# Routing of 15 of 16 token tiles moved from the expert stage into the last attention chunks of a one-core layer

## The reference

```
xn = layernorm(x) * gamma + beta
w = sigmoid(xn @ Wx @ Ww + bw); k = xn @ Wk; v = xn @ Wv; r = sigmoid(xn @ Wr)   # 8 heads of 64
state_t = (1 - w_t) * state_{t-1} + k_t v_t^T ;  y_t = r_t^T state_t
x1 = layernorm(x + y @ Wo)
logits = x1 @ gate_w.T                                  # 12 experts
top_w, top_i = top_k(softmax(logits), 2); top_w /= sum(top_w)
out = layernorm(x1 + sum_e  silu(x1 @ w1[e].T) * (x1 @ w3[e].T) @ w2[e].T * cw[:, e])
```

## Time and profile before

| | us |
|---|---|
| median of three runs | 822.91 (820.64 to 826.37) |
| the profiled execution, its own time | 822.39 |
| its span, first to last instruction | 820.5 |
| PE busy in the span | 730.4 (89%) |
| DVE, ACT, POOL busy | 501.1, 342.5, 312.5 |
| mean granted TensorE clock | 0.959 of full speed |

### The profile page before, as it was taken

One profiled execution on the slowest core, in us unless ns is written; L12 is line 12 of the kernel. 1 busy time (PEld: TensorE's weight loads), 2 busy tenths in 40 slices (PEclk: granted clock), 3 DMA queues, 4 the chain that ended last, 5 costly groups with the idle time before them and its releaser, 6 DMA issues. The chain is left out here.

```text
span 820.5 us, 17687 instructions
## 1 busy us (share of the span) xinstructions
PE 730.4 (89%) x6146; PEld 523.5 (64%) x6147; DVE 501.1 (61%) x1061; ACT 342.5 (42%) x688; POOL 312.5 (38%) x341
## 2 busy tenths in 40 slices
PE   5879899999999999999959971499999999999994
PEld 2658587886878868788636621366666666666641
DVE  4735968768587685876855558444444443444467
ACT  4455544646446464564375321122222222222254
POOL 0337554344554444544443102233443433444210
PEclk9999999999999999999969986699999999999997
DMA  8604443334433354323540249125555555722865
GB/s 341 248 2 155 154 154 105 104 104 155 155 104 104 103 156 155 116 91 104 154 154 29 76 148 364 51 66 192 185 191 187 192 201 208 265 79 89 274 251 205
DMA packets 39001, 126.64 MB, mean 154 GB/s; under 512 B 4000, under 2 KB 4384, under 8 KB 36768
## 3 DMA queue, kind: packets, MB, share of 16 engines
q1 hardware_dynamic: 32064, 103.31, 36.2%
q0 software_dynamic: 6880, 22.55, 8.2%
HBM read 81.02 MB, written 44.83 MB: 153 GB/s over the span
## 5 line engine op out<-in xcount | busy, mean ns | idle before, releaser
L854 DVE COPY_PREDICATED ST<-msk,pS 128x256 f32<-128x256 uint8 x224 | 121.1, 570 | 80.4 <-issue 51.1
L589 POOL TENSOR_TENSOR piece_parts<-piece,piece_parts 128x1024 f16<-128x1024 f32 x48 | 103.9, 2164 | 104.0 <-ACT piece_parts L534 104.0
L583 POOL TENSOR_TENSOR L<-L,AM 128x256 f32<-128x256 f32 x96 | 73.8, 769 | 109.4 <-ACT L L526 104.6
L1282 PE MATMUL pH<-ring,xgh 128*128 x344 | 104.2, 303 | 5.5 <-issue 3.0
L1283 PE MATMUL pH<-ring,xgh 128*128 x344 | 103.9, 302 | 0.0
L1284 PE MATMUL pH<-ring,xgl 128*128 x344 | 103.9, 302 | 0.0
L306 PE MATMUL pS<-L 64*128 64x64 f32 x1536 | 96.3, 271 | 0.0
L1616 POOL DMA_INDIRECT y_scratch<-ysb,sidx x43 | 42.9, 998 | 135.5 <-DVE ysb L1532 130.0
L1516 DVE TENSOR_TENSOR hid<-pH,sil 128x320 f32<-128x320 f32 x43 | 21.1, 492 | 119.5 <-ACT sil L1368 119.5
L567 DVE TENSOR_TENSOR L<-L,AM 128x256 f32<-128x256 f32 x96 | 72.8, 759 | 31.5 <-ACT L L513 29.9
L306 PEld LDWEIGHTS pS<-L 64*128 64x128 f32 x1536 | 91.1, 188 | 0.0
(11 more groups left out here) (239 smaller groups left out, 1673.5 us busy)
## 6 DMA issues: line engine op xcount, KB each, us to landing
piece<-in_w_experts SPq DMA_DIRECT2D x48, 512.0 KB, 5.1
w_split_scratch<-piece_parts SPq DMA_DIRECT2D x48, 512.0 KB, 3.9
ring<-w_split_scratch SPq DMA_DIRECT2D x12, 2048.0 KB, 8.7
yin<-y_scratch SPq DMA_DIRECT2D x16, 512.0 KB, 13.3
x_scratch<-X SPq DMA_DIRECT2D x1, 4096.0 KB, 14.4
out_x<-X SPq DMA_DIRECT2D x8, 512.0 KB, 2.8
X<-in_x SPq DMA_DIRECT2D x1, 3072.0 KB, 22.9
X<-in_x SPq DMA_DIRECT2D x2, 512.0 KB, 7.7
```

Source lines behind the costliest of these rows:

```text
L583: g.tensor_tensor(next_kept(k, lv, 0), kept(key, k, lv, 0), by, ALU.mult).then_inc(k_dec, 1)
L589: g.tensor_tensor(piece_parts[buf][:, 1, :], piece[buf][:, :], piece_parts[buf][:, 0, :], ALU.subtract).then_inc(piece_lo, 1)
L854: v.copy_predicated(out[:, :, :, 0 if lv == 0 else 1, :], msk[:, lv, :, :].rearrange(shape, m=m), pS[:, :, lv * S:(lv + 1) * S].rearrange( ...
L1282: pe.matmul(p[:, 0, 0:F], xgh[par][:, k, :], wh, start=(k == 0), stop=False)
```

## The change

1. `early`, a memory area of 32 KB for each partition, is shared: it holds the z and k weights first, then the routing's arrays (class `Routing`), later the diagonals of the mixing. pA lives through both blocks.
2. Weight pieces: 4 for each of chunks 0 to 11 (`LOT = 4`, pieces 2 and 3 both after level 6) and none in 12 to 15. ACT casts the fourth at the end of the chunk.
3. x1 is normalised in more and earlier parts (`X1_PARTS`): the root of tiles 0 to 7 at the end of chunk 9, their norms at the ends of chunks 10, 11, 12; tiles 8 to 11 in chunk 13, 12 in 14, 13 and 14 in 15. Each tile is stored by a DMA that ACT issues behind the next norm. Tile 15 is stored in the expert block.
4. Gating: the gate weights are padded to 32 columns and the four feature groups go to four column groups of PE side by side; a second step ("sum") adds them and gives the logits by token. Tiles 12 to 14 are gated alone with x as weights ("direct"). All 24 steps stand in chunks 13 to 15.
5. The top two of tiles 0 to 14 are found by DVE in chunks 14 and 15, the counts by PE behind chunk 15 (ahead of its `attend_out`), the ranks by DVE, and POOL makes 15 column one-hots at the end of the block.
6. The last chunk's state update, with `turn_keys` and `write_state`, is left out; its result is not used.
7. In the expert block only tile 15 is routed; the token number is multiplied into the column one-hots, one instruction for each tile and choice. Running sums of the tiles by expert come from one product and one reduction. The first four gathers use the address table in place.

```diff
-PIECE_AT = (4, 5, 6)
+PIECE_AT = {4: (0,), 5: (1,), 6: (2, 3)}
+UNITS = [u for q in range(3) for u in [("turn", q * GROUP + r) for r in range(GROUP)] + [("gate", q), ("sum", q)]]
+UNITS += [u for i in range(3 * GROUP, NT - 1) for u in (("turn", i), ("direct", i))]
+GATE_SLOTS = {NT - 3: [[0, 1], [2, 3], [4, 5, 6], [7, 8], [9, 10]], NT - 2: [[11], [12, 13], [14, 15], [16], [17, 18, 19]],
+              NT - 1: [[20], [21], [22, 23], [], []]}
+X1_PARTS = [(0, 8), (8, 12), (12, 13), (13, 14), (14, 15), (15, 16)]
+LATE_NORMS = {10: (0, 3), 11: (3, 6), 12: (6, 8)}
+NORM_SLOTS = {NT - 3: [range(8, 9), range(9, 11), range(11, 12)], NT - 2: [range(12, 13), [], []]}
-LOT = 3
+LOT = 4
+PIECED = 12
...
@@ PE, gate_step(u) @@
+                pe.wait_ge(gate_out, u - 1 if kind == "turn" and 2 <= u < SINGLE else u)
+                elif kind == "gate":
+                    for k in range(KT):
+                        t = pe.matmul(pA[GATE_W * k:GATE_W * (k + 1), bank, :], gw[:, k, :], xT[:, k, :], start=True, stop=True)
+                elif kind == "sum":
+                    for r in range(GROUP):
+                        t = pe.matmul(pA[:, bank, r * E:(r + 1) * E], logitT[:, r * P:(r + 1) * P], kc_col(kc, K_SUM),
+                                      start=(r == 0), stop=True, skip_group_check=True)
...
+            def count_tokens():
+                pe.wait_ge(gate_out, SINGLE)
+                pe.wait_ge(chosen_ready, 4)
+                pe.matmul(pA[:, 1, 0:(NT - 1) * E], ro.upper_h, ro.chosen[:, 0:NT - 1, :].rearrange("p n e -> p (n e)"),
+                          start=True, stop=True, skip_group_check=True)
+                for m in range(NT - 1):
+                    later = NT - m
+                    t = pe.matmul(pA[:, 1, (m + 1) * E:(NT + 1) * E], ro.ones_h,
+                                  ro.chosen[:, m:m + 1, :].broadcast_to([P, later, E]), start=False, stop=True, skip_group_check=True)
+                t.then_inc(count_full, 1)
...
+            count_tokens()
             attend_out(NT - 1)
...
@@ ACT, norm and chunk @@
+                if t:
+                    send_x2(t - 1)
+            def send_x2(t):
+                a.wait_ge(norm2, t + 1)
+                a.dma_start(x2_d[t * P:(t + 1) * P, :], X[:, t, :]).then_inc(x2_out, 16)
...
                 fill(4)
+                split(3)
+                if n == 9:
+                    root_x1(0)
+                if n in LATE_NORMS:
+                    a.wait_ge(stat2, 3)
+                    for t in range(*LATE_NORMS[n]):
+                        norm(t)
...
@@ DVE, chunk @@
+                if n == NT - 1:
+                    top_two(8, 12)
                 mask(n, k, 0)
...
                     add_out(n - 1)
+                if n == NT - 2:
+                    top_two(0, 4)
                 level(3)
...
+                if n == NT - 2:
+                    top_two(4, 8)
...
+            top_two(12, NT - 1)
             low_y(NT - 1)
+            ranks()
             add_out(NT - 1)
...
@@ POOL, end of the attention block @@
+            g.wait_ge(ranked, 1)
+            for n in range(NT - 1):
+                i = g.tensor_scalar(ro.oh_col[:, n, :], ro.col_h, ro.colf[:, 0, n:n + 1], tokens[:, n:n + 1], ALU.is_equal, ALU.mult)
...
@@ expert block, SP @@
-            sp.dma_start(x2_d.rearrange("(n p) c -> p n c", p=P), X[:, :, :]).then_inc(x2_out, 16)
+            sp.dma_start(x2_d[last * P:, :], X[:, last, :]).then_inc(last_out, 16)
...
@@ expert block, DVE (the four groups of tiles and L1435 to L1466 go) @@
+            v.tensor_copy(slot_h[:, :], kcol(K_SLOT))
+            columns(1, 0, last)
+            v.wait_ge(gate_full, 1)
+            step(v.tensor_copy(ro.logit[:, last, :], pO[:, 0, 0:E]))
+            step(v.max(ro.top[:, last, :], ro.logit[:, last, :]))
...
+            step(v.tensor_reduce(place[:, :, :], placed[:, :, :, :], AX.X, ALU.add))
+            columns(0, last, NT)
+            columns(1, last, NT).then_inc(col_ready, 1)
+            step(v.tensor_tensor(tile_h[:, :].rearrange("p (c n) -> p c n", c=2), place[:, :, :], ro.tilf[:, :, :], ALU.add))
+            for c in range(2):
+                at = slice(c * NT, (c + 1) * NT)
+                v.tensor_tensor(oh_tile[:, at, :], slot_h[:, :].rearrange("p (o n) -> p o n", o=1).broadcast_to([P, NT, SLOTS]),
+                                tile_h[:, at].rearrange("p (n o) -> p n o", o=1).broadcast_to([P, NT, SLOTS]), ALU.is_equal).then_inc(tile_ready, 1)
...
+            v.wait_ge(list_full, 1)
+            v.tensor_scalar(toki[:, :], pHT[:, 0, 0:SLOTS], -1.0, 0.0, ALU.add, ALU.max).then_inc(list_ready, 1)
...
@@ expert block, POOL @@
-            g.wait_ge(tile_ready, 1)
-            g.tensor_tensor(oh_tile[:, :, :], oh_tile[:, :, :],
-                            kcol(K_TOKEN, kh).rearrange("p (o n) -> p o n", o=1).broadcast_to([P, 2 * NT, SLOTS]),
-                            ALU.mult).then_inc(numbered, 1)
             g.wait_ge(list_ready, 1)
-            for k in range(AHEAD):
-                fetch(k, k, k + 1, first=True)
+            for k in range(AHEAD):
+                g.sem_inc(g_waited, 1)
+                g.indirect_dma_start(out=xg[k][:, :], out_offset=None, in_=x2_d,
+                                     in_offset=bass.IndirectOffsetOnAxis(ap=toki[:, k:k + 1], axis=0)).then_inc(x_in[k], 16)
```

More of the change, by code:

```diff
@@ L1243, in _ @@
-            for m in range(NT):
-                later = NT - m
-                t = pe.matmul(pG[:, 0, (m + 1) * E:(NT + 1) * E], ones[:, :],
-                              chosen[:, m:m + 1, :].broadcast_to([P, later, E]), start=False, stop=True, skip_group_check=True)
-            t.then_inc(count_full, 1)
-            pe.wait_ge(numbered, 1)
+            for k in range(KT):
+                t = pe.transpose(pX[:, 0, k * P:(k + 1) * P], X[:, last, k * P:(k + 1) * P], idt[:, :])
+            t.then_inc(gate_T, 1)
@@ new lines, in _ @@
+            pe.wait_ge(gate_T_out, 1)
+            for k in range(KT):
+                t = pe.matmul(pO[:, 0, 0:E], xT[:, k, :], gw[:, k, 0:E], start=(k == 0), stop=(k == KT - 1))
+            t.then_inc(gate_full, 1)
+            pe.wait_ge(last_chosen, 1)
+            for at, w in ((last, ro.upper_h), (NT, ro.ones_h)):
+                t = pe.matmul(pG[:, 0, at * E:(at + 1) * E], w, ro.chosen[:, last, :], start=False, stop=True, skip_group_check=True)
+            t.then_inc(total_full, 1)
+            pe.wait_ge(col_ready, 1)
@@ L1254, in _ @@
             t.then_inc(list_full, 1)
+            for n in range(NT, 2 * NT):
+                t = pe.matmul(pH1[:, 0, 0:SLOTS], ro.oh_col[:, n, :], oh_tile[:, n, :], start=(n == NT), stop=(n == 2 * NT - 1))
+            t.then_inc(second_full, 1)
             def turn(i, k, rounds):
@@ new lines, in _ @@
+            v.tensor_tensor(ro.chosen[:, last, :], ro.onehot[:, 0, last, :], ro.onehot[:, 1, last, :], ALU.add).then_inc(last_chosen, 1)
+            v.wait_ge(total_full, 1)
+            block_of = [pG[:, 0, i * E:(i + 1) * E].rearrange("p (o e) -> p o e", o=1) for i in (last, NT)]
+            v.tensor_tensor(ro.picked[:, :, last, :], ro.onehot[:, :, last, :], block_of[0].broadcast_to([P, 2, E]), ALU.mult)
+            step(v.tensor_scalar(counti[:, :], pG[:, 0, NT * E:(NT + 1) * E], float(P - 1), None, ALU.add))
@@ new lines, in _ @@
+            v.tensor_scalar(ro.tili[:, :, last:], ro.sloti[:, :, last:], P.bit_length() - 1, None, ALU.logical_shift_right)
+            step(v.tensor_reduce(tbase[:, :], before[:, :, :], AX.X, ALU.add))
+            v.tensor_copy(ro.colf[:, :, last:], ro.coli[:, :, last:])
+            base = tbase[:, :].rearrange("p (o e) -> p o e", o=1).broadcast_to([P, NT, E])
+            for c in range(2):
+                v.tensor_tensor(placed[:, c, :, :], ro.onehot[:, c, :, :], base, ALU.mult)
+            step(v.tensor_copy(ro.tilf[:, :, last:], ro.tili[:, :, last:]))
@@ L1594, in _, with fetch @@
         def _(g):
[L1596 to L1599 removed]
+            def fetch(i, k, steps):
+                g.wait_ge(xt_full, i - (AHEAD - 1))
                 g.tensor_copy(gidx[k][:, :], toki[:, bass.ds(i, 1)]).then_inc(g_step, 1)
```

487 lines of the change are left out of this document (251 added, 236 removed).

## The result

The changed kernel took 829.84 us in the median of 11 runs (827.81 to 835.01), the kernel before 822.91 in the median of 11 beside them. The ratio is 1.0088, with a 95% interval from 1.0057 to 1.012. The forecast was 812.7, in a range of 800 to 824: it had the kernel faster, and it became slower than the whole range. The profiled execution of the changed kernel took 831.66 us, its span 829.5, 9.0 more than the span of before.

What follows compares the result with a forecast made beforehand. PE was taken to bound the middle chunks (busy 273.4 of 280 us), a DVE chain the routing. The terms 10.0 - 1.9 + 2.7 - 20.5 = -9.7 against the profiled 822.4 us gave 812.7, range 800 to 824.

Steps and rivals of the forecast that it cites:

- fourth piece, up to chunk 13: Chunks 0 to 11: the extra weight piece delays chunk 0, odd chunks and chunk 11; PE pays 10.0 us before chunk 13.
- chunks 13 to 15, up to the mask: Chunk 13 wins 8.5 us, chunk 14 gives 6.6 back, chunk 15 keeps its length: last mask 1.9 us earlier.
- block's end: After the last mask: POOL's 15 column one-hots at 0.35 us each delay the routing; cost 2.7 us, upper bound 9.
- routing: Start of the expert block: with only tile 15 left, 40.4 us without expert matmuls become 19.9, a gain of 20.5.
- the walk: The prediction's step-by-step adding up of work and waits through the engines' queues, in the chunks and the routing.
- All of it shifts by 3.1: Chunk 0: the fourth cast delays wo_h and wo_l, level 0, key copy, kbT and PE's values by 3.1 us, bounds 0 and 3.5.
- the forecast of 0.8 each: Chunks 1, 3, 5, 7, 9: the extra cast delays kbT, for which PE already waits; 4.1 us in all, bounds 0 and 6.
- no wait of PE there is over 2 us: Chunks 13 to 15: PE's waits stay short, where before they were 3 to 4 us; argued against the clock falling.
- The gate of four column groups: Gating in chunks 13 to 15: each group overlaps only its neighbour's second pass, so 2.2 us a gate, bounds 0.9 and 3.6.
- The feared loss to DVE: Block's end: by the shared-port lock, POOL's columns can lose some 1.5 us to DVE, making the sum 814.2.
- Rival 3: Chunks 13 to 15: the clock falls to 1.2 GHz, 19 us more, 831.7 and slower than before; chance 0.10.
- Rival 2: Routing gain partly eaten at both ends: POOL columns at 0.6 (+3.7), gather held by ring loads (+3); 819.4; chance 0.20.

Runs made afterwards that it cites:

- e8: Changed kernel, but SyncE loads the third expert's weights into the ring only after the first gather of tokens has landed; one run took 830.71 us.
- e2: Changed kernel with three weight pieces in chunk 0, four in chunks 1 to 11 and one in chunk 12; 826.91 us, ratio to before 1.0045.
- e1: Changed kernel again, with only the loaded counts kept as 16-bit numbers and one short DVE step added; 828.79 us, ratio to before 1.0082.
- e9: Changed kernel, but in chunk 0 PE turns the same keys seven more times before reporting them, to stay busy in its wait; one run took 823.95 us.
- e6: Changed kernel with three weight pieces in all 16 chunks; 820.32 us, ratio to before 1.0009.
- e11: As e10, but a fourth weight piece only in even chunks from 2 to 12 and no pieces in chunks 14 and 15; 797.48 us, ratio to before 0.9693.
- e7: Changed kernel, but the second turn of the gating (unit 1) doesn't wait for ACT's copy of unit 0; one run took 822.46 us.
- e5: Changed kernel, but in chunk 14 the third gate and its sum precede the second half's values; tile 12's direct gate moves to chunk 15; 820.65 us, ratio 0.9994.
- e4: Changed kernel, but in chunk 14 PE writes the state update three more times while waiting for the second mask; 829.34 us, ratio to before 1.0077.
- e10: Changed kernel with the edits of e6, e7, e5 and e8, and the column one-hots shared between POOL and DVE; 816.61 us, ratio to before 0.9947.

## Why the prediction was wrong, step by step

Predicted and measured against the span of before, in us. T and T' are the ends of the last mask, as in the prediction: 474.98 and 494.20.

```
                                  predicted   measured
fourth piece, up to chunk 13         +10.0      +15.4
chunks 13 to 15, up to the mask       -1.9       +3.8
block's end                           +2.7       +9.0
routing                              -20.5      -18.8
rest                                     0       -0.5
sum                                   -9.7       +9.0
```

**Routing: near.** `toki` came 12.07 us after the block's start, the walk said 12.1; `oh_tile` at 9.05, the walk had 8.7. What was short is the gather: from its issue to the first expert matmul 8.4 instead of 7.2. e8 gives a part of the cause: without the third ring load the gather was 2.1 shorter and the first matmul 0.8 earlier. The walk had charged the ring loads with 0.5 us.

**Fourth piece: mechanism right, size too small, one effect left out.** "All of it shifts by 3.1": in e2 against e1 it was 4.3. The fourth cast began 5.67 us after its load was issued (64.42, then 70.09); the walk's 70.5 allows 4.7, less than its own row of 5.1. With its row the shift would have been 3.5; it was 4.0 on ACT and 4.3 behind POOL. The step that failed is that nothing was said of what PE does behind the wait: 3.8 us of clock in chunk 0.

In the odd chunks the forecast of 0.8 each was near: PE's wait for kbT went to 1.43 in chunks 1, 3, 5 and 7, and chunks 1 to 8 lost 2.2 together. (The five waits of before that the walk counted, in 120 to 400 us, are those of chunks 3 to 11 and not 1 to 9; the sum is the same.) For chunk 9 it was wrong by its clock. There PE waited 2.24 us for kbT, and of the 12 matmuls of `attend_out` eight then ran 0.43 apart instead of 0.22: 4.36 us from the first to the values, 2.68 in e9 where the wait was 1.45. For chunk 11 the walk had 2.8, and chunks 10 and 11 together lost 3.4: the late `normalise` that it foresaw came (the wait of 1.82 us at 365.67), and some 1.6 of the 3.4 are the clock behind that wait, by eight transposes and `read_state` at the low level. e6 and e11 show the late norms to be nearly free where chunk 11 has three pieces.

**Chunks 13 to 15: the step that failed is the walk's "no wait of PE there is over 2 us".** There were two, of 3.04 and 3.45 us. The first comes from a condition that I had in the diff before me and read as meant, not as written: for `u = 1` it falls through to `else u`. The first turn's copy stands on ACT behind kbT, three key copies and four state operations. e7 gives its price, 4.5 us; as chunk 13 even so won 7.4 of the 8.5 forecast, other terms of the walk there were too dear, and which is open. The second I had seen as a wait for the mask, but not that it stands in front of four units. I put 28.5 us from first mask to first mask for chunk 14, and it was 32.49 (446.55 to 479.04): 4.0 of the 5.7 by which this line of the table is off. e5 shows that the order alone, with the clock that comes with it, is worth 11.6.

The gate of four column groups was the one term on the other side: 1.06 us at the high level, 1.94 at the low, where I took 2.2. Eight passes with all 512 columns had taken 3.60, so the groups overlap 3.4 times. The Trainium skill (TensorEngine Tiling (Array Packing), "Theoretical Speedup") allows up to 4; by that rule a gate is 0.9, an estimate, and the trace is near it. My estimate from half-width passes was wrong by a factor of two. Its formula gave 0.70 for them where the row has 0.66; two groups side by side in full would give 0.60, and that reading was nearly as good.

**Block's end: the column was mis-sized.** I took 0.35 us, with 0.77 as the upper bound "its dearest short form"; it is 0.78, and with that price the prediction's own bound, 9, is what was measured (9.0). It was not contention with DVE: the 15 took 784 ns in the median and 783 at least, and those behind 504.18, when DVE had nothing to do, took no less. The feared loss to DVE (1.5 us, by the lock of the shared port) was not there: the dearest of the 15 took 857 ns.

**Rivals.** Rival 3, the clock, gave 831.7 and had 0.10; the profiled run took 831.66. That the numbers agree is chance: the clock cost an estimated 16 us (3.8 in chunk 0; 1.7 in chunk 9; 1.6 where chunk 11 begins; 1.7 in chunk 13, where eight matmuls of `attend_out` came 0.43 apart instead of 0.22; some 7.5 in chunk 14, 3.3 by e4 for the units and 4.2 against e5 for the scores and `read_state` of chunk 15), and only half of it stood where rival 3 had it. Not all of it is new: the kernel before had a low stretch of its own in 400 to 435 us, at 0.76. Rival 2, both ends dearer, held in part: the block's end cost 6.3 more than forecast, where it had 3.7, and the gather 1.2, where it had 3. The signs given for both came: a clock under 0.9 in 435 to 483 us, and a first gather of 5.66 us from issue to landing. What I took for rivals were parts of one sum. The chance was put on one of them at a time.

## What to carry to other kernels

A wait of PE has two prices: its length and, as after five waits of 1.82 to 5.38 us in the changed kernel, the 1.2 GHz level for the work behind it. Put what PE can do in front of a wait and not behind it; here, moving two units across one wait and a third into the next chunk was worth 11.6 us of a chunk, and one needless condition 4.5. Work that is "free" on a half-empty engine (weight pieces on ACT) was free here only in those chunks where no other engine waited for that engine in turn: the same 48 pieces, dealt out otherwise, were the difference between 816.6 and 797.5 us. And before a row of small operations is given to an engine that has no row for them, take the dearest bound and see whether the plan still holds.

## What was unexpected of the hardware

- POOL took 0.78 us for a 128x128 fp16 comparison with two per-partition scalars, DVE 0.23. That is more than POOL's multiply of 128x256 fp32 at its fastest (0.61).
- A wait's length alone didn't tell what PE's clock did behind it. In the changed kernel it fell after waits of 1.82, 2.24, 3.04, 3.45 and 5.38 us. It stayed up after 2.25 (e9, chunk 0), after 2.31 (before, chunk 0), where it fell after 2.32 in e2, and after 3.03 at the second turn of chunk 13 in e6. In e4 and e11 it fell in chunk 14 where no wait was over 0.82. Two waits at one place can end both ways: in chunk 9 of the changed kernel it fell after 2.24 and the chunk took 28.9; in e7 it stayed up after 2.23, and it took 27.2. Why PE waits 2.2 us there in some executions and 1.45 in others (e9) stays open.

```profile
314.39 0.39 PE L417 MATMUL pM<-wo_h,yTh 128*128 128x512 f16 x1 [2.24 <-ACT kbT L805]
```

```profile
312.83 0.38 PE L417 MATMUL pM<-wo_h,yTh 128*128 128x512 f16 x1 [2.23 <-ACT kbT L805]
```

The first is the changed kernel, the second e7.
- In e10 a DVE cast of 8 elements a lane took 1.79 us, where its three like took 0.16 to 0.17 (in e6 one took 1.79 too), and ended at 445.14, when POOL's subtraction ended (445.11):

```profile
442.98 2.13 POOL L668 TENSOR_TENSOR piece_parts<-piece,piece_parts 128x1024 f16<-128x1024 f32 x1 [3.50 <-ACT piece_parts L613]
...
443.35 1.79 DVE L1044 CAST early<-early 128x8 f32<-128x8 uint32 x1
```

By the Trainium skill (SBUF — State Buffer, "SBUF: two separate sides") POOL and a DVE operation that is in a fast two-port mode, or has two SBUF inputs, exclude each other, and whichever starts first holds the shared ports for its whole instruction. The prediction had only POOL as the one that waits; here DVE waited, and the trace agrees with the rule that way round too, though no row shows in which mode this cast ran.
